# The second projection of a graph attention layer in two column passes, with the logit vectors as two more columns of the weights

## The reference, cut to what matters

```
x = x + GNN(layernorm(x))                 # 1250 nodes x 768; 20000 edges and the self loops
x = x + FFN(layernorm(x)[None])[0]        # router, 8 experts and a shared one, 768 -> 384 -> 768

def GNN(x):   h1  = elu(gat(x,  W1, concat, 4 heads of 512))       # 1250 x 2048
              out = gat(h1, W2, 1 head of 768)                     # 1250 x 768
def gat(x, W, a_src, a_dst, b):
    h = x @ W
    al_s, al_d = h . a_src, h . a_dst                              # logits: 2 numbers a node
    e = leaky_relu(al_s[src] + al_d[dst], 0.2)
    alpha = exp(e - max_over_dst(e)) / sum_over_dst(...)
    return segment_sum(h[src] * alpha, dst) + b
```

## Time and profile before

| | us |
|---|---|
| median of 3 runs (1324.44 to 1327.47) | 1326.48 |
| the profiled execution's own time | 1322.85 |
| its span, first to last instruction | 1321.1 |
| busy in the span: TensorE / VectorE / ScalarE / GpSimd | 1207.5 / 873.4 / 609.4 / 161.9 |
| mean granted TensorE clock | 0.967 |

### The profile page before, as it was taken

One profiled execution on the slowest core, in us unless ns is written; L12 is line 12 of the kernel. 1 busy time (PEld: TensorE's weight loads), 2 busy tenths in 40 slices (PEclk: granted clock), 3 DMA queues, 4 the chain that ended last, 5 costly groups with the idle time before them and its releaser, 6 DMA issues.

```text
span 1321.1 us, 18384 instructions
## 1 busy us (share of the span) xinstructions
PE 1207.5 (91%) x7111; PEld 802.9 (61%) x7111; DVE 873.4 (66%) x1766; ACT 609.4 (46%) x1108; POOL 161.9 (12%) x144
## 2 busy tenths in 40 slices
PE   4887778888999799999999999999998799999996
PEld 3665443444555455545788888888556566666664
DVE  7889879988997899898543652444786323333330
ACT  5679356476546554876403650102311144444441
POOL 1000000000000000000000004000103734333322
PEclk9998999988999899999999999998999899999999
DMA  8344530462145323412753206213201587677532
GB/s 185 125 143 145 147 97 20 122 164 81 44 129 158 89 57 102 124 36 78 267 158 103 78 15 178 70 41 102 72 1 47 160 225 180 171 177 181 162 63 32
DMA packets 70210, 149.66 MB, mean 113 GB/s; under 512 B 10629, under 2 KB 34693, under 8 KB 69498
## 3 DMA queue, kind: packets, MB, share of 16 engines
q1 hardware_dynamic: 63467, 131.23, 33.2%
q0 software_dynamic: 6656, 17.26, 6.8%
HBM read 115.88 MB, written 34.59 MB: 114 GB/s over the span
## 4 chain that ended last, share of the span: by engine, by line
PE 58%; DVE 21%; issue 6%; ACT 6%; DMA 4%; SPq 2%; POOL 2%; POOLq 0%; DVEq 0%; ACTq 0%
PE PS L1775 47%; PE PS L1918 6%; DVE sb L1421 3%; DVE sb L1400 3%; DVE sb L1436 2%; DVE sb L1429 2%; SPq L541 2%; DVE sb L1288 1%; DVE sb L1470 1%; DVE sb L1371 1%; DVE sb L1481 1%; DMA sb<-aa_d 1%; POOL sb L850 1%; DMA sb<-in_L_ffn_w_dram 1%; DVE sb L1317 1%
## 5 line engine op out<-in xcount | busy, mean ns | idle before, releaser
L1775 PE MATMUL PS<-sb,sb 128*125 128x384 f16 (+8 forms) x4404 | 780.5, 337 | 45.3 <-DVE sb L1293 27.0
L1775 PEld LDWEIGHTS PS<-sb,sb 128*125 128x125 f16 (+3 forms) x4404 | 541.0, 128 | 269.0 <-issue 55.6
L1918 PE MATMUL PS<-sb,sb 125*128 125x375 f16 (+1 forms) x1440 | 263.1, 343 | 0.0
L1918 PEld LDWEIGHTS PS<-sb,sb 125*128 125x128 f16 x1440 | 140.5, 98 | 119.7 <-issue 9.5
L1619 DVE SCALAR_TENSOR_TENSOR sb<-sb,sb 128x2304 f16<-128x2304 f32 x27 | 68.8, 2557 | 84.5 <-ACT sb L1143 84.5
L1016 ACT ACTIVATE sb<-sb 125x375 f32<-125x375 f32 (+1 forms) x150 | 81.4, 543 | 83.6 <-DVE sb L1421 83.2
L830 POOL TENSOR_TENSOR sb<-sb,sb 125x768 f32<-125x768 f32 x10 | 18.0, 1838 | 803.2 <-DMA sb<-in_x_dram 803.2
L1421 DVE SCALAR_TENSOR_TENSOR sb<-sb,sb,sb 125x375 f32<-125x375 f32 (+1 forms) x150 | 95.6, 638 | 5.6 <-ACT sb L1010 5.4
L1010 ACT ACTIVATE sb<-sb,sb 125x375 f32<-125x375 f32 (+1 forms) x150 | 93.7, 628 | 0.7 <-DMA sb<-aa_d 0.7
L1429 DVE SCALAR_TENSOR_TENSOR sb<-sb,sb 125x375 f32<-125x375 f32 (+1 forms) x150 | 87.7, 585 | 1.2 <-ACT sb L1016 1.1
L1436 DVE TENSOR_TENSOR sb<-sb,sb 125x375 f16<-125x375 f32 (+1 forms) x150 | 87.9, 586 | 0.1
(11 more groups left out here) (188 smaller groups left out, 1062.0 us busy)
## 6 DMA issues: line engine op xcount, KB each, us to landing
sb<-in_L_ffn_w_dram SPq DMA_DIRECT2D x24, 1152.0 KB, 5.7
sb<-in_L_gnn_W_dram SPq DMA_DIRECT2D x32, 384.0 KB, 4.6
sb<-xt_d SPq DMA_DIRECT2D x30, 375.0 KB, 4.9
sb<-mask_d SPq DMA_DIRECT2D x20, 546.9 KB
sb<-h_d SPq DMA_DIRECT2D x10, 1000.0 KB, 5.4
h_d<-sb SPq DMA_DIRECT2D x16, 375.0 KB, 4.8
sb<-aa_d SPq DMA_DIRECT2D x5, 1093.8 KB
h_d<-sb SPq DMA_DIRECT2D x8, 500.0 KB, 5.0
```

What stands on the lines that cost most here:

```text
L1775: ins = M(out_, lhs(a), rhs(b), start=first and a + b == 0, stop=last and a == 1)
L1918: ins = M(PS[:, t, 0:n], hb[:, i, pa, 128 * c:128 * c + 128], P[:, i, pb, lo:lo + n], start=i == 0 and pa + pb == 0, stop=i == NT - 1 and ...
```

## The change

v2's halves become two more columns of every W2 chunk, so a chunk is 770 columns wide: 2 of v2, 768 of W2. The second projection runs over the tiles twice. The first pass takes columns 0 to 321 (v2 and the first 320 of W2), the second the other 448; each pass has 10 tiles x 16 chunks x 3 matmuls. The logits of a tile are columns 0 and 1 of its first pass, and `h2_lo` scales them straight from PSUM. All of `al2`, `al2_columns`, their semaphores, the wait of ScalarE and SP on them, and DVE's 12 x 500 copy go. DVE writes v2's halves into the chunks, one 128 x 2 x 2 copy ahead of each `w2_lo`.

The tiles of h1 lie in 8 buffers, five of them in P's room, which is free between the last group of layer 1 and P's first steps of layer 2. The second pass takes the tiles as 9, 2 to 8, 0, 1; tiles 0 and 1 are loaded a second time. `chain_row` moves to the second pass, first tile, chunk 4; `chain_shift` to its fourth tile, chunk 8. `P2_STEPS` gives P's rounds as 5, 5, 5, 5, 5, 0 ahead of the takes of units 14 to 19, and 7 behind unit 19. P's high halves for block 0 wait for the units that free their room. Banks rotate over six halves instead of three pairs; units 0 and 1 use banks 6 and 7, units 2 to 5 wait for the last four `att_read`.

```diff
-    W2S = [at(o_w2s + 3072 * i, [128, 2, D], F16) for i in range(9)]
-    HT = [at(o, [128, 2, NCH, T], F16) for o in (o_t, o_h1, o_h1 + 8000, o_y)]
+    W2S = [at(o_w2s + W2B * i, [128, 2, D + 4], F16) for i in range(9)]
+    HT = [at(o, [128, 2, NCH, T], F16) for o in (o_t, o_h1, o_h1 + 8000)]
+    HT += [at(o_p + 8000 * i, [128, 2, NCH, T], F16) for i in range(5)]
...
+        HALF_B = [9, 2, 3, 4, 5, 6, 7, 8, 0, 1]
+        HT_SLOT = [0, 1, 3, 4, 5, 6, 7, 2, 1, 0, 2, 1]
+            return (6, 7, 0, 1, 2, 3)[u % 6]
-        P2_STEPS = [0, 0, 0, 0, 6, 6, 6, 6, 6, 2]
+        P2_STEPS = [0] * (NT + 4) + [5, 5, 5, 5, 5, 0, 7]
+        DA = 320
...   load_ht on SP
+                elif v == 2:
+                    sp.wait_ge(s_att, NG * H)
+                elif v == 6:
                     sp.wait_ge(s_h1s[(NB * H - 1) % 2], 32 * ((NB * H - 1) // 2 + 1))
+                elif v >= 8:
+                    sp.wait_ge(s_pj2, (2, 1, NT + 7, NT + 8)[v - 8])
...   ScalarE
+                if h == H and b == 0:
+                    act.wait_ge(s_pj2, NT + 2 + min(4, (4 * N * i + 4 * N - 1) // 8000))
-                A(W2S[ch][:, 0, :], W2G[u % 3][:, :], ACT.Copy, scale=SW).then_inc(s_w2h, 1)
+                A(W2S[ch][:, 0, 2:D + 2], W2G[u % 3][:, :], ACT.Copy, scale=SW).then_inc(s_w2h, 1)
...   VectorE
+                V.tensor_copy(W2S[ch][:, :, 0:2], V2S[:, ch, :, :])
+                    V.tensor_scalar(AL[:, :, H, j], PS[0:T, bank2(u), 0:2], 1.0 / (SX * SW), None, ALU.mult
+                                    ).then_inc(s_a2r, 1)
+            for u in range(NT):
+                h2_lo(u)
+            chain_row(H)
+            for u in range(NT, NT + 3):
+                h2_lo(u)
+                for j in range((0, 4, 8)[u - NT], (4, 8, NT)[u - NT]):
+                    chain_max(H, j)
             chain_shift(H)
...   TensorE
-                    if c == CH - 1 and NB * h + b:
-                        al2(NB * h + b - 1)
-            for j in range(NT):
+            for u in range(2 * NT):
...
+                if 2 <= u < 6:
+                    pe.wait_ge(s_y1, CH * NB * H - 5 + u)
+                if u >= 6:
+                    pe.wait_ge(s_h2l, h2_made(u - 6))
                 for ch in range(NCH):
-                    if j == 0:
+                    if u == 0:
                         pe.wait_ge(s_w2l, ch + 1)
-                        if ch == 12:
-                            al2(NB * H - 1)
-                    for q in range(2):
-                        ins = mm3(PS[0:T, b + q, 0:DH], lambda a: ht[:, a, ch, :],
-                                  lambda r: W2S[ch][:, r, DH * q:DH * q + DH], ch == 0, ch == NCH - 1)
+                    if u == NT and ch == 4:
+                        chain_row(H)
+                    if u == NT + 3 and ch == 8:
+                        chain_shift(H)
+                    ins = mm3(PS[0:T, b, 0:part.stop - part.start], lambda a: ht[:, a, ch, :],
+                              lambda r: W2S[ch][:, r, part], ch == 0, ch == NCH - 1)
```

More of the change, by code:

```diff
@@ L134, in build @@
     assert o <= 207008, o
-    A2W = at(o_a - 2016, [12, 500], F32)
     XA = at(o_y, [T, NT, D], F32)
@@ L428, in step, with half_tile, ht_use @@
             return NT * (NB * h + b) + i
[L430 to L432 removed]
+        HALF_A = list(range(NT))
+        HALF_B = [9, 2, 3, 4, 5, 6, 7, 8, 0, 1]
+        HT_SLOT = [0, 1, 3, 4, 5, 6, 7, 2, 1, 0, 2, 1]
+        def half_tile(u):
+            return (HALF_A + HALF_B)[u]
+        def ht_use(u):
+            v = half_tile(u) if u < NT or half_tile(u) >= 2 else NT + half_tile(u)
+            return HT[HT_SLOT[v]], s_ht[v % 4], 16 * (v // 4 + 1)
         def v2_in(ch):
@@ L820, in _ @@
             link(nc.gpsimd.memset(big[:, :], -NEG))
-            link(nc.gpsimd.memset(SEL[:, :, :], 0.0))
-            for part in range(2):
-                link(nc.gpsimd.affine_select(out=SEL[:, :, :], in_=SEL[:, :, :], compare_op=ALU.not_equal, fill=1.0,
-                                             base=-2 * part, pattern=[[-4, NB], [-1, 2]], channel_multiplier=1))
             pool.wait_ge(s_bias, 48)
@@ L1575, in _ @@
                                    ).then_inc(s_wl, 1)
-            h2_lo(0)
-            for j in range(NT):
-                chain_max(H, j)
+            for u in range(NT):
[5 more added lines that the diff above has]
+                    chain_max(H, j)
             chain_shift(H)
-            h2_lo(1)
             chain_shift_rows(H)
-            for j in range(2, NT):
-                p_steps(H, P2_STEPS[j])
-                h2_lo(j)
+            h2_lo(NT + 3)
+            for u in range(NT + 4, 2 * NT):
+                p_steps(H, P2_STEPS[u])
+                h2_lo(u)
+            p_steps(H, P2_STEPS[2 * NT])
             def x2t_lo(i):
@@ L1923, in att @@
                 ins.then_inc(s_att, 1)
-            def al2(k):
-                h, b = divmod(k, NB)
-                n, nj = DB[b][1], len(TB[b])
-                pe.wait_ge(s_y6, CH * (k + 1))
-                if k in (0, NB * (H - 1)):
-                    pe.wait_ge(s_vs, 1 if k == 0 else 2)
-                for c in range(CH):
-                    for part in range(2):
-                        ins = M(PS[0:12, 4, 0:n], V2S[:, CH * h + c, 8 - 4 * b:20 - 4 * b],
-                                H1O[k % 2][:, part, 0:nj, c, :], start=k + c + part == 0,
-                                stop=k == NB * H - 1 and c == CH - 1 and part == 1)
-                ins.then_inc(s_a2, 1)
-            def al2_columns():
-                pe.wait_ge(s_const, 16)
-                pe.wait_ge(s_a2r, 1)
-                for b in range(NB):
-                    for j in TB[b]:
-                        lo = T * (j - TB[b].start)
-                        ins = M(PS[0:T, 5, 2 * j:2 * j + 2], A2W[:, lo:lo + T], SEL[:, b, :], start=True, stop=True)
-                ins.then_inc(s_a2c, 1)
             for h in range(H):
@@ L1999, in _ @@
                 b = 4 + 2 * (j % 2)
-                for i in range(NT):
+                order = HALF_B if j == 0 else HALF_A
+                for i in order:
                     if j == 0:
-                        pe.wait_ge(s_h2l, 3 * (i + 1))
+                        pe.wait_ge(s_h2l, h2_made(NT + HALF_B.index(i)))
                     for b_ in range(NB):
```

157 lines of the change are left out of this document (70 added, 87 removed).

## The result

The changed kernel takes 1334.18 us (median of 20 runs), the kernel before 1324.99 us on the same chip; the ratio is 1.007, 95% interval [1.0054, 1.0086]. It is slower, by 9.2 us of the medians. The profiled executions stand 10.9 us apart, 1321.1 and 1332.0 us of span. Eighteen of the changed kernel's twenty executions took 1331.6 to 1340.2 us, the other two 1320.66 and 1325.57; only one of the long ones was profiled, so what made those two short isn't known. The forecast was 1329.6 us, or +3.8 worked out: the sign and the wide range hold, but the forecast's own band, 1327.5 to 1332, doesn't, and more than half of the loss came from a place where the forecast saw 4 us of cover.

A forecast was written before the change was run, and what follows sets the result against it. TensorE was taken to bound the second projection, with VectorE ending last at layer 1's head changes. 7.6 us saved against 8.5 + 2.0 + 0.4 + 0.6 lost gave about +3.8 on 1326.48; forecast 1329.6, range 1321.5 to 1335.5.

The forecast's parts named there:

- the sign: Whole kernel: the change makes it slower, chance 0.53.
- the wide range: Whole kernel: measured time between 1321.5 and 1335.5 us.
- the forecast's own band: Whole kernel: 1327.5 to 1332 us if the forecast alone holds.
- 4 us of cover: End of the logit chain: second attention's first normalised tile ready at E + 107.3, wanted by TensorE at E + 111.4.
- The new wait in unit 0: Start of second projection: TensorE waits for W2's last low halves, so unit 0 ends at 654.2, not 645.7; 8.5 us.
- the copies: VectorE's path to W2's last chunk: 16 small copies of v2's halves add 1.5 us, bounds 0 and 2.2.
- The rival without this wait: Unit 0: TensorE gets W2 as fast as it wants it; -6.7 us, 1319.8, chance 0.17.
- The clock behind it: Units 1 and 2 of the second projection: half clock after TensorE's idleness loses 2.0 us, bounds 0 and 3.
- the pricing of narrow matmuls by columns: Second projection: 0.424 ns a column, so 136.6 ns at 322 columns and 190.0 at 448.
- Layer 1: Dropping layer 1's eleven `al2` groups saves 0.8 us, bounds 0 and 15, most being hidden in waits for VectorE.
- The second attention's start: Behind the second projection's two passes: start at 807.2 instead of 803.5, +3.7 us.
- later P: P's last 7 rounds: end 7 us later through slower rounds or late shift rows; +7 us, 1333.5, chance 0.13.

The follow-up runs named there:

- e3: Changed kernel with unit 0 reading W2's first nine chunks over and over, so it waits for no late low half (wrong result); ratio 1.0023 to the kernel before.
- e4: Kernel before with each `al2` of layer 1 but the last cut from 8 matmuls to 1; 1322.01 us, ratio 0.9974 to the kernel before.
- e7: Kernel before with GpSimd's ten bias additions cut to 8 of 768 columns; ratio 0.999 to the kernel before.
- e10: Changed kernel with all W2 halves made ahead of VectorE's last attention read, P's last seven rounds still late; ratio 1.003 to the kernel before.
- e8: Kernel before with P's last seven rounds moved behind the last tile of the second projection; ratio 1.0078 to the kernel before.
- e1: Changed kernel with five of P's last seven rounds ahead of unit 19's take and two behind it; ratio 1.0029 to the kernel before.
- e2: Changed kernel with GpSimd's ten bias additions cut to 8 of 768 columns, P's rounds still late; ratio 1.001 to the kernel before.
- e6: Changed kernel with the edits of e1 and e3 together; ratio 0.9951 to the kernel before.
- e5: Changed kernel with e1's early rounds and W2's halves made one attention group sooner in layer 3; ratio 1.0031 to the kernel before.
- e9: Changed kernel with e1's early rounds and all W2 halves made ahead of VectorE's last attention read; ratio 1.000 to the kernel before.
- e11: e9 with units 0 and 1 interleaved, the last three chunks of each coming last; 1320.65 us, ratio 0.9971 to the kernel before.

## Why the prediction was right or wrong

- **The new wait in unit 0** is there, at L1524, as the forecast said, in three pieces (0.32, 3.90, 0.38) and not two. The waits add up to 4.6 us. The 8.5 of the forecast were the whole delay of unit 0's end, its matmuls at the low clock included; measured like that it is some 6.0 (without a wait 640.45 + 6.6 = 647.1; with it 652.4 and three matmuls, near 653.1). The projection started at 640.45 and not 639.1, so the chunks were wanted 1.3 us later. And the last low half came at 652.4 and not 653.4, partly because the copies cost 0.07 to 0.08 us from start to start, 1.2 us in all and not 1.5. The rival without this wait (1319.8) did not occur.
- **The clock behind it**: 0.50 in 652:654, as said. The row of e3 at full clock holds 432 matmuls of 322 columns and 12 of 448 in 61.53 us, so (61.53 - 12 x 0.1905) / 432 = 137.1 ns for 322 columns. Six more make 62.35, and the changed kernel's row has 64.01: 1.7 us, forecast 2.0. Widths: 137.1 and 190.5 ns, forecast 136.6 and 190.0; the pricing of narrow matmuls by columns was right.
- **Layer 1** gave 0.85 us at the projection's start in the profile. Over the three profiles with all the eights the start is 641.4 on average (641.30, 640.16, 642.85), over the nine without them 640.9, between 639.1 and 642.4. The term, 0.8, can't be told more closely from that; e4's 3.4 us [1.2, 5.6] says that it may be more. That it is not 15 is shown. In the changed kernel TensorE is idle 36.4 us from 212 to 641 us, before 28.3: 8.1 us of the 15 are waited out, 4.5 of them at head 3's change, and the rest stands where its granted clock is lower. The forecast had the waits and not the clock. The row at head 3's change in the changed kernel, then the last stretch of layer 1 before and after (columns: stretch, its length, TensorE's busy time, PEclk, DMA share, GB/s):

```profile
442.95 33.02 PE L1797 MATMUL PS<-sb,sb 128*125 128x512 f16 x144 [12.09 <-DVE sb L1315]
```
```profile
561.00:641.00 80.00, 76.82 (x425) 0.98 0.30 95
561.00:641.00 80.00, 76.26 (x406) 0.93 0.31 96
```

- **The second attention's start** was put at +3.7 and came at +1.5: the over-sized wait. The first pass took 72.6 us (640.45 to 713.1) and not 76.1.
- **The step that failed** is the last of the logit chain: "4 us of cover remain". The place of the rounds was right (25 rounds ended at 799.08, 86 us behind E = 713.1, which is 715.4 less 12 matmuls of unit 10; forecast 90; the last seven began with the last take). At their usual pace they would have ended near E + 101.6; the forecast had E + 102. But their duration was taken from the earlier trace rows, where GpSimd is idle. Beside the additions six of their instructions and the normalising step took 10.6 us more, so they ended at E + 111.1, and the tile was ready at E + 116.9 where the forecast had E + 107.3. 5.5 us of wait and 2.9 us of clock came of it, 8.4 of the 10.9. The forecast asked where the moved rounds stand in time but not what GpSimd does then; in the trace before, the additions and the normalising step of 1.50 us beside them (817.10, L1610; 0.68 in e7, the same kernel without them) were to be seen. The rival "later P" (chance 0.13, 1333.5 us) is the nearest to what happened, by its size and its place. It named another reason for the lateness, and that reason was not at work. That 1334.18 lies in the wide range is luck in part: the range reached that far for this rival's sake, and an over-sized wait (2.2 us too much at the second attention's start) hid part of the 8.4 us that the forecast lacked.

## What to carry to other kernels

Where a change moves work in time, list what every engine does in the new stretch, GpSimd too, and take durations from a stretch where the same neighbours run. A wait of TensorE for 4 to 6 us costs its length and, behind it, some more at half clock: 1.7 us behind 3.90 and 2.9 behind 5.46 in the changed kernel, but 1.7 behind 5.46 in e10 (transposes 1.51, row of 60 at 10.96), and 2.3 behind 6.07 in e8. When a rewrite loses by a few tenths of a per cent, undo its side effects one by one before judging the idea: here two tables of steps and an order of chunks took the ratio from 1.007 to 0.997.

## What the hardware showed

- VectorE's instructions with two inputs in SBUF go from 0.55 to 2.15 us while GpSimd adds two 125x768 fp32 tiles, one instruction of VectorE to one addition (starts 2.07 apart). One with an input in PSUM (0.62 at 824.61) and the statistics with one input (1.02 for two at 825.91) keep their length in the same stretch. The normalising step, one tile and two numbers a row from SBUF, goes from 0.68 to 1.88. GpSimd's ten additions go from 18.03 to 20.36 us. The Trainium skill (SBUF — State Buffer, section "SBUF: two separate sides") describes this as an exclusive lock on a shared pair of ports, held for a whole instruction, for operations of VectorE with two SBUF inputs (against a GpSimd operation that reads SBUF) or in a two-port mode; by that rule the loser waits out one addition, and the trace agrees: 1.6 us more an instruction against some 1.8 us for one addition (18.03 / 10). GpSimd can be the loser too: in e8 its first addition, from 811.11, took 3.14 us, while VectorE's instructions with two SBUF inputs kept their usual 0.54 to 0.60 us until 812.50.
- Profiles of the same code differ by as much as the effects looked for. In five kernels that are equal up to the projection (changed, e1, e2, e3, e6) its start lies between 639.55 and 642.35; in five that are equal from the first x2 transposes on and don't wait there (e1, e5, e6, e9, e11) the rest takes 498.4 to 502.8 us. What makes it differ was not tried. The start-to-start time inside the changed stage, where equal stages agree within 0.6 us (181.6, 182.2 and 182.2 for before, e4 and e7), told the mechanisms apart where whole times could not.
